# Node degrees of three chunks from the step tables instead of from products with a column of ones (graph network, one core)

## The reference

```
agg  = segment_sum(x[src], dst, num_segments=n)
deg  = segment_sum(ones_like(dst), dst, num_segments=n)
mean = agg / maximum(deg, 1)[:, None]
x    = mean @ Wl + x @ Wr + b
```

## Time and profile before

| what | us |
|---|---|
| median of 3 runs (lowest, highest) | 658.54 (657.63, 659.53) |
| the profiled execution's own time | 655.78 |
| its span in the profile | 653.9 |
| VectorE busy (share of the span) | 273.1 (42%) |
| ScalarE busy | 178.8 (27%) |
| layer 1: round 0 begins | 46.9 |
| round 1 begins | 102.8 |
| round 2 begins | 123.3 |

### The profile page before, as it was taken

How to read it: one execution, slowest core, us unless ns; L and a number is a source line. 1 busy time by engine, 2 the same in 40 slices (tenths; PEclk the granted TensorE clock), 3 DMA queues, 4 the chain that set the end, 5 groups by cost and what they waited for, 6 DMA issues and landing times.

```text
span 653.9 us, 10056 instructions
## 1 busy us (share of the span) xinstructions
PE 619.4 (95%) x4059; PEld 344.1 (53%) x4060; DVE 273.1 (42%) x514; ACT 178.8 (27%) x381; POOL 42.4 (6%) x93
## 2 busy tenths in 40 slices
PE   5769998899999899999999999899999999999998
PEld 4445555565555445554444444444446555646686
DVE  6978867589798779711121121121110110100011
ACT  3896853364644513210021011211110000000000
POOL 8003100000000000000000000000010011010110
PEclk9968999899999999999999999999999999999999
DMA  8401201510221112442435341355430213032030
GB/s 262 101 2 51 77 1 48 152 40 6 69 49 46 35 43 66 50 137 65 145 92 155 82 124 40 74 145 124 112 114 1 76 49 113 2 111 92 21 113 33
DMA packets 63526, 50.98 MB, mean 78 GB/s; under 512 B 35511, under 2 KB 48348, under 8 KB 63481
## 3 DMA queue, kind: packets, MB, share of 16 engines
q1 hardware_dynamic: 63124, 49.74, 27.0%
q0 software_dynamic: 240, 0.37, 0.2%
q10 hardware_dynamic: 116, 0.24, 0.1%
HBM read 28.15 MB, written 16.60 MB: 68 GB/s over the span
## 4 chain that ended last, share of the span: by engine, by line
PE 77%; DMA 8%; DVE 5%; ACT 5%; issue 2%; SPq 2%; POOL 1%; DVEq 0%; ACTq 0%; POOLq 0%
PE agg_ps L2254 27%; PE window_ps L2254 18%; PE lin_ps L2172 6%; PE lin_ps L2189 5%; PE window_ps L2085 4%; PE lin_ps L2148 3%; DMA rdeg_d<-newH 3%; PE lin_ps L2042 2%; DMA rdeg_d<-rdeg 2%; PE window_ps L2230 2%; PE agg_ps L2230 2%; ACT counts L1807 2%; DMA newH<-rdeg_d 1%; PE lin_ps L2276 1%; PE lin_ps L2197 1%
## 5 line engine op out<-in xcount | busy, mean ns | idle before, releaser
L2254 PE MATMUL agg_ps<-counts,H 128*128 128x512 f16 (+3 forms) x1026 | 234.9, 355 | 0.9 <-DVE aggT L1550 0.8
L2254 PEld LDWEIGHTS agg_ps<-counts,H 128*128 128x128 f16 (+1 forms) x1026 | 79.1, 98 | 55.9 <-issue 10.1
L1807 ACT ACTIVATE counts<-window_ps 128x400 f16<-128x400 f32 x150 | 73.6, 507 | 64.4 <-PE window_ps L2085 49.6
L1452 DVE TENSOR_TENSOR counts<-early 128x2048 f16<-128x2048 bf16 x66 | 78.0, 1215 | 6.6 <-PE window_ps L2085 5.1
L2254 PE MATMUL window_ps<-counts,early 128*128 128x512 f16 (+2 forms) x346 | 77.6, 379 | 0.0
L2254 PEld LDWEIGHTS window_ps<-counts,early 128*128 128x128 f16 (+1 forms) x346 | 33.7, 98 | 41.5 <-issue 3.4
L2254 PE MATMUL window_ps<-counts,H 128*128 128x512 f16 (+2 forms) x291 | 55.3, 346 | 0.0
L1550 DVE SCALAR_TENSOR_TENSOR aggT<-agg_ps,columns,rdeg 128x512 f32<-128x512 f32 (+1 forms) x27 | 17.0, 659 | 79.8 <-PE agg_ps L2254 63.1
L2085 PEld LDWEIGHTS window_ps<-counts 128*128 128x128 f16 x412 | 30.7, 99 | 34.6 <-issue 4.7
L1452 DVE TENSOR_TENSOR early<-early 128x1024 f16<-128x1024 bf16 (+1 forms) x69 | 43.9, 684 | 6.8 <-PE window_ps L2085 5.4
L2254 PE MATMUL agg_ps<-counts,early 128*128 (+4 forms) x297 | 46.5, 314 | 0.0
(11 more groups left out here) (251 smaller groups left out, 640.7 us busy)
## 6 DMA issues: line engine op xcount, KB each, us to landing
selfT<-hT_d SPq DMA_DIRECT2D x18, 512.0 KB, 4.3
hT_d<-newT SPq DMA_DIRECT2D x12, 512.0 KB, 4.5
rdeg<-rdeg_d SPq DMA_DIRECT2D x22, 256.0 KB, 4.2
counts<-in_x_dram SPq DMA_DIRECT2D x6, 512.0 KB, 7.9
hT_d<-counts SPq DMA_DIRECT2D x6, 512.0 KB, 3.3
newH<-in_x_dram SPq DMA_DIRECT2D x6, 512.0 KB
out_dram<-newT SPq DMA_DIRECT2D x5, 512.0 KB
hT_d<-newT SPq DMA_DIRECT2D x6, 256.0 KB, 4.0
```

Source lines behind the costliest of these rows:

```text
L1452: v.tensor_tensor(hots_of(group).rearrange("p r a (n d) -> p r a n d", d=2), pairs.unsqueeze(1).unsqueeze(1).broadcast_to([P, n, 2, P // 2 ...
L1807: a.activation(counts[:, :, 2 * w * WIN:2 * (w + 1) * WIN].rearrange("p t (a w) -> p a t w", a=2), window_bank(FILL_AT[w])[:, 0:2 * KEYS]. ...
L2254: last = m((agg_ps, window_ps)[bank][:, h, 0:n], tile[:, part, h * P:(h + 1) * P], counts[0:rows_, k, chunk_cols(c, n)], start=first and p ...
```

## The change

Places 0 to 2 take the way of the others: their degrees come from the step tables too. `add_degrees`, `degrees`, `turn_degrees` and `copy_degrees` are removed. The comparisons of place 0 are made at the start of round 0 and summed at its index 1, those of places 1 and 2 late in round 0, into rows of `counts` that are free then. The row now has one partition only (partition 32 of the `plan` tile), and all seven chunks are stored as a row and loaded as four neighbouring nodes on a partition, so that a piece has 16 bytes (4 bytes for the chunk of 53 nodes). `rdeg` is loaded only when the sums of the place before have been scaled. On SyncE the way of place 0 goes between the first h0 stores, that of place 1 to the head of `after(0)`, and that of place 2 into `after(1)`. GpSimd clears the row where it cleared `rdeg`.

```diff
-    BY_STEPS = 3
+    FROM_PARTS = 3
+        degree_row = plan_all[32:33, :].bitcast(f32)
...
+        early_cuts = [row(19, CH, CUT_SLOT), row(19, CH + CUT_SLOT, WTAIL * (WIN + 1)), row(20, CH, CUT_SLOT)]
...
-                def turn_degree_row(q):
...
+                def store_degree_row(q):
+                    c = ORDER[q]
+                    n, t = size_of(c)
+                    sp.wait_ge(degrees_taken, q + 1)
+                    sp.dma_start(rdeg_d[0:1, c * CH:c * CH + n], row_of(q)).then_inc(degree_row_stored, 16)
+                    sp.wait_ge(degree_row_stored, 16 * (q + 1))
+                    sp.dma_start(rdeg_columns[0:n // t, q, 0:t], degree_columns(q)).then_inc(degree_columns_loaded, 16)
+                def degree_columns(q):
+                    c = ORDER[q]
+                    n, t = size_of(c)
+                    return rdeg_d[0, c * CH:c * CH + n].rearrange("(p t) -> p t", t=t)
+                def store_rdeg(q):
+                    n, t = size_of(ORDER[q])
                     sp.wait_ge(degree_inverted, q + 1)
+                    sp.dma_start(degree_columns(q), rdeg_columns[0:n // t, q, 0:t]).then_inc(rdeg_columns_stored, 16)
+                    sp.wait_ge(rdeg_columns_stored, 16 * (q + 1))
+                    if q > 0:
+                        sp.wait_ge(agg_scaled[1], 2 * q)
+                    c = ORDER[q]
+                    sp.dma_start(rdeg[:, 0:n], rdeg_d[0:1, c * CH:c * CH + n].broadcast_to([P, n])).then_inc(rdeg_back, 16)
...
                     if l == 1 and not last:
                         double_tail(q + 1)
+                        if q == 0:
+                            store_degree_row(1)
+                            store_rdeg(1)
...
                         store_new(q)
-                        if l == 1 and BY_STEPS <= q + 1 < NCH:
-                            turn_degree_row(q + 1)
+                        if l == 1 and 2 <= q + 1 < NCH:
+                            store_degree_row(q + 1)
+                            store_rdeg(q + 1)
...
                     double_tail(0)
-                    for j in range(3):
+                    for j in range(2):
                         store_h0T(j)
+                    store_degree_row(0)
+                    store_h0T(2)
+                    store_rdeg(0)
                     load_self(0)
...
-                    sp.wait_ge(degree_inverted, BY_STEPS)
-                    for q in range(BY_STEPS):
-                        store_rdeg(q)
...
+            g.memset(degree_row, 0.0).then_inc(row_cleared, 1)
+            pool.wait_ge(row_cleared, 1)
...
-                    dve.wait_ge(rdeg_back, 16 * (q - BY_STEPS + 1)) if q >= BY_STEPS else dve.wait_ge(rdeg_made, q + 1)
+                    dve.wait_ge(rdeg_back, 16 * (q + 1))
...
-            first_round = {0: lambda: (h0_moments(3), bases_late(2)), 1: lambda: (degrees(0), h0_low_part(2)),
+            first_round = {0: lambda: (cut_steps(0), h0_moments(3), bases_late(2)), 1: lambda: h0_low_part(2),
+                           2: lambda: take_degrees(0),
...
+                           12: lambda: h0_low_part(4), 13: lambda: h0_shift(5), 14: lambda: invert_degrees(0),
+                           15: lambda: h0_low_part(5), 17: lambda: (cut_steps(1), cut_steps(2)),
...
-            second_round = {0: bound_h1, 2: bound_h2, 3: lambda: (add_own(0), plan_low()), 4: bound_h3, 15: lambda: low_part(1, 0, 0),
+            second_round = {0: lambda: (take_degrees(1), bound_h1()), 2: bound_h2, 3: lambda: (add_own(0), plan_low()),
+                            4: lambda: (bound_h3(), invert_degrees(1)), 15: lambda: low_part(1, 0, 0),
...
             def turn_bases():
                 pe.wait_ge(bases_made, 1)
+                pe.wait_ge(degrees_taken, 1)
...
-            def add_degrees(q):
...
-            def turn_degrees(q):
...
+            first_round = {1: lambda: sum_cuts(0), 3: lambda: turn_bases(), 4: lambda: h0_turn(2), 7: lambda: own_products(2),
...
-                if q < BY_STEPS:
-                    add_degrees(q)
-                else:
-                    if q < NCH - 1:
-                        sum_cuts(q)
+                if 0 < q < NCH - 1:
+                    sum_cuts(q)
+                if q > 1:
                     pe.wait_ge(low_done[1], q - 1)
...
                     if q == 1 and k == H0_LATE_K:
-                        pe.wait_ge(rdeg_made, 1)
+                        pe.wait_ge(degrees_taken, 2)
```

More of the change, by code:

```diff
@@ L985, in _ @@
                 after(1)
-                if l == 1:
-                    for q in range(2, NCH - 2):
-                        after(q)
-                    sp.wait_ge(degree_inverted, BY_STEPS)
-                    for q in range(BY_STEPS):
-                        store_rdeg(q)
-                elif l < 4:
+                if l < 4:
                     for q in range(2, NCH - 2):
@@ L1093, in _ @@
                                          ).then_inc(rows_gathered[i], 16)
-            for q in range(BY_STEPS, NCH):
-                pool.wait_ge(agg_scaled[1], 2 * q)
-                g.memset(rdeg[:, :], 0.0).then_inc(rdeg_cleared, 1)
+            for q in range(2, NCH):
+                pool.wait_ge(degree_row_stored, 16 * (q if q > 2 else 1))
+                g.memset(degree_row[:, 0:CH], 0.0).then_inc(row_cleared, 1)
             pool.wait_ge(late_loaded, LATE)
@@ L1504, in note @@
+                    v.tensor_reduce(out=degree_row[:, (CH if place == 1 else 0):][:, bass.ds(at, WIN)],
+                                    in_=degree_ps[32:33, 0:KEYS].rearrange("p (t w) -> p w t", w=WIN), axis=AX.X,
                                     op=ALU.add).then_inc(heavy_noted, 1)
                 for c in DUE[q]:
-                    if ORDER.index(c) < BY_STEPS:
-                        heavy_windows(dve, c, regs, rounds)
-                    else:
-                        heavy_windows(dve, c, regs, lambda w, first, n: (rounds(w, first, n), note(c, w)))
+                    heavy_windows(dve, c, regs, lambda w, first, n: (rounds(w, first, n), note(c, w)))
@@ L1636, in _ @@
                         first_round[k]()
-                    if 1 <= q < BY_STEPS and k == DEGREE_K:
-                        degrees(q)
-                    if BY_STEPS <= q + 1 < NCH - 1 and k == CUT_AHEAD_K:
+                    if FROM_PARTS <= q + 1 < NCH - 1 and k == CUT_AHEAD_K:
                         cut_steps(q + 1)
@@ L1861, in high_part @@
                     act.wait_ge(narrow_done, q + 1)
-                    if q + 1 >= BY_STEPS and q + 1 < NCH:
-                        act.wait_ge(cuts_summed, q + 2 - BY_STEPS)
+                    if FROM_PARTS <= q + 1 < NCH:
+                        act.wait_ge(cuts_summed, q + 2)
                 else:
@@ L1937, in _ @@
                         continue
-                    if k == DEGREE_COPY_K and q < BY_STEPS:
-                        copy_degrees(q)
                     if k == RELU_K:
@@ L2294, in sum_cuts @@
                 last.then_inc(cuts_summed, 1)
-            def turn_degrees(q):
-                n, t = size_of(chunk_at(q))
-                rows_ = P if n == CH else n
-                pe.wait_ge(degree_inverted, q + 1)
-                if q >= 1:
-                    pe.wait_ge(rdeg_made, q)
-                for i in range(t):
-                    last = m(degree_ps[:, i * P:i * P + rows_], rdeg_columns[0:rows_, q, i:i + 1].broadcast_to([rows_, P]),
-                             ident32[0:rows_, 0:rows_], start=True, stop=True)
-                last.then_inc(degree_turned, 1)
             def pick_rows():
@@ L2365, in _ @@
                     if kind == "lin":
+                        if q == 1 and k == 0:
+                            pe.wait_ge(own_copied, 2 * IN_LIN)
                         lin_part(q - 1, k)
```

161 lines of the change are left out of this document (56 added, 105 removed).

## The result

The changed kernel takes 666.88 us (median of 4 runs, 666.24 to 667.27), the kernel before 659.03 beside it (4 runs, 657.63 to 660.96): ratio 1.0118, interval 1.009 to 1.0146. It is slower, by 7.85 us, and the time lies above the range.

A forecast was written before the change was run, and what follows sets the result against it. TensorE was taken to set the pace, busy 619.4 of 653.9 us. Terms +2.6 + 0.5 - 0.9 - 1.3 + 0.8 = +1.7 us on the median 658.54 gave 660.2; range 654.5 to 665.

The forecast's parts named there:

- The price of the 53-piece store: SyncE, round 1: column store of 53 4-byte pieces takes 3.1 us at 13 ns a piece, bounds 2.45 and 10.45.
- second rival: SyncE's queue, round 1: small store costs by the transfer, 7.9 us, round 2 begins 4.8 later, 666.3 us; chance 0.18.
- Round 0: Products and turning go, VectorE's first one-hot pair sets the start: round 1 begins 1.6 us earlier, bounds 0.9 to 3.8.
- The fourth h0 store: SyncE ahead of round 2: first store lands in 3.0 us, three more add 3.8, fourth landed at 126.5.
- Round 1 up to the inversion: VectorE: bound operations run 13.6 us without a break from 101.75; inversion behind them done at 115.5.
- The clock after the stand: TensorE, start of round 2: half rate after standing some 8 us costs 0.5 us more, between 0 and 1.6.
- Rounds 2 to 6: Later rounds: turning goes -0.9, late-store waits go -1.3, round 2 waits for its columns +0.8 us.
- The turning: TensorE, round 2: turning a degree column into a row goes, -0.9 us.
- both go: -1.3: TensorE waits of 0.7 in round 4 and 0.6 at the last inversion vanish with shorter column stores; bounds 0 and -2.5.
- The 0.8 that round 2 was to get: Round 2: VectorE stands before the inversion until columns are back, costing TensorE +0.8 us, 0 to 1.5.
- first rival: Round 2 start: h0 stores in time, removed products' time comes out, sums begin 5.0 earlier, 652.1 us; chance 0.2.
- third rival: Rounds 0 to 2: windows with too many edges would run their own counts now; no change; chance 0.02.

The follow-up runs named there:

- row_before_h0: Changed kernel with only the degree row of place 0 stored ahead of the h0 of places 0 to 2: 663.88 us, ratio 1.0039.
- pieces_of_16: Changed kernel with place 1's degrees moved as 14 pieces of 16 bytes instead of 53 of 4 bytes: 661.39 us, ratio 0.9987.
- both edits: Changed kernel with place 1 as 14 pieces of 16 bytes and its inverted-degree store behind the four h0 stores: 654.11 us, ratio 0.9875.
- layout-alone kernel: Kernel before, with only the columns of places 3 to 6 as four neighbouring nodes a partition; products with ones stay: 656.78 us, ratio 0.9938.
- inverted_early_16: Changed kernel with 14 pieces of 16 bytes for place 1, its inversion before the first self addition, place 0's row before h0: 652.79 us, ratio 0.9809.

## Why the prediction was wrong, point by point

The path up to round 2's first sum and its order were right. That sum came 10.0 us later than forecast, through four terms that were sized too small (9.6 together; the rest is mostly the 2.9 from the landing to the sum, forecast 2.6). The length behind it, -1.1 us for a forecast of -0.9 (+0.5 - 0.9 - 1.3 + 0.8), agrees by luck.

**The price of the 53-piece store: 3.1 forecast, 6.4 measured (+3.3).** The step that failed is "by the piece, ... 13 ns". The price isn't linear in the pieces: 53 and 64 of 4 bytes cost 6.4 each, 512 cost 7.9 to 10.5, and 14 or 128 of 16 bytes 1.3 to 1.4. So "near the single piece, as 53 is nearer 1 than 512" interpolated between two points of which one, the single row of 2 KB, was of another kind. This is the second rival, with its place, its threshold (over 3.4 us) and its time, 666.3, close to 666.88. That closeness is luck: it held 4.8 for the store, which cost 3.3, and nothing for the three terms below. And its second half, that the new stores of 128 pieces stay slow too, was wrong. With that goes the rule that was weighed there (the Trainium skill, DMA: Bandwidth & Descriptors, "Specifications", a read-modify-write below 512 B): as the only rule it would make 4 and 16 bytes alike, and here they differ by a factor of 4 to 5. The other rounds' stores took 1.4 to 2.5 from issue to next issue in the changed kernel, instead of the forecast's 4.2.

**Round 0: 1.6 earlier forecast, 1.1 later measured (+2.7).** VectorE's first pair set the start, as forecast (50.15 for 49.6). The step that failed is the one from there to "round 1 begins 1.6 earlier": behind the first pair the next wait was ScalarE's, because its register load took 3.19 instead of at most 1.27 beside the h0 stores. The prediction had bounded this term by VectorE alone and had not asked what the earlier first sum releases on SyncE. With the stores moved (row_before_h0) round 1 begins at 101.79, 1.05 before the old 102.84: two thirds of the 1.6. The other third, with the degree products at half clock as forecast, was not split further.

**The fourth h0 store: 6.8 after the first issue forecast, 9.05 measured (+2.25).** The step that failed is "one such store lands in 3.0 at the least". That row was of stores issued far apart. Four in a row share the queue from the start; the first takes 5.2, which was the upper end of the earlier trace rows and the bound that the prediction named, and 5.2 + 3 x 1.28 is 9.04. With pieces_of_16 the first took 4.3, and the fourth landed at 8.2, again 3 x 1.28 more. The upper bound was the row of the same kind: it belongs to the pair issued 0.6 us apart at the start of round 0. That other stores behind them lengthen it was tried and is not so. The changed kernel's DMA issue of 127.10, last number from issue to landing, and its line 793 over all seven stores:

```profile
hT_d<-counts SPq DMA_DIRECT2D x1, 512.0 KB, 5.2
```

```profile
DMA to landing us min/median/max: 3.2/5.2/6.9
```

**Round 1 up to the inversion: 14.3 forecast, 15.6 measured (+1.3).** The step that failed is that the bounds run "without a break" for 13.6: TensorE ran at its lower level at the start of round 1, and VectorE waited for its products.

```profile
111.90 0.69 DVE L1584 TENSOR_TENSOR newT<-lin_ps,selfT 128x512 f32<-128x512 f32 x1 [0.85 <-PE lin_ps L2155]
```

Stretches as in the earlier trace rows; the third one is round 2's start:

```profile
105.00:108.00 3.00, 3.00 (x16) 2.94 (x16) 2.26 (x6) 1.17 (x3) 0.00 (x0) 0.50 0.05 7
...
130.00:136.00 6.00, 0.00 (x0) 0.00 (x0) 0.00 (x0) 0.00 (x0) 0.00 (x0) 0.50 1.03 394
...
139.00:142.00 3.00, 2.94 (x14) 1.56 (x15) 1.60 (x3) 0.87 (x2) 0.00 (x0) 0.50 0.27 98
```

At full clock the new round 1 takes what was forecast: with both edits (eight h0 transposes in 1.09 us) it is 14.3 from its begin to the inversion (105.05 to 119.39). The low clock isn't peculiar to the change. The layout-alone kernel, with the old round 1, shows it too (1.97), and two kernels with the new one don't (the one with both edits, and inverted_early_16). But nine of the eleven traces with the new round 1 have some of it between 100 and 110, and one of the two with the old; whether the change makes it more frequent was not tested. The execution profiled before had full clock there. The span grew by 11.5 and the median by 7.85 because that execution lay 3.25 below its median and the one profiled after 0.4 above; how much of the 3.25 is the clock isn't shown.

**The clock after the stand: +0.5 forecast, nothing to be seen.** TensorE stood for 13.7 us, the granted clock was 0.50 by 130, and it stayed at 0.50 for 3 us of work, until 142; before, it was some 3.4 us of 126 to 130. A longer stand did not make the start slower. The trace agrees with the Trainium skill (TensorE: Matmul & The Clock Gate, "What's actually happening"): "the default state is throttled, and activity releases the throttle".

**Rounds 2 to 6: -1.4 forecast (-0.9 - 1.3 + 0.8).** The turning came out as forecast: from round 2's first sum to the degree products of round 3 it is 33.7 us (139.06 to 172.8), before 34.7 (126.46 to 161.20). The step that failed is "both go: -1.3". Both waits stand in the changed kernel, as long as before:

```profile
PE turn_ps L2087 <- DVE early L1471: 0.7, 1, 0.7
PE lin_ps L2155 <- DVE aggT L1571: 0.6, 1, 0.6
```

The layout-alone kernel has them too, so the late stores weren't their cause; what is was not tried. The 0.8 that round 2 was to get has no wait in the trace, and round 3's 0.8 went. So up to the first sum of round 6 the changed kernel took 2.05 less (126.46 to 274.95 before, 139.06 to 285.50 now). Round 6 gave 1.7 of this back up to its wait of 0.6 (274.95 to 306.22, and 285.50 to 318.46), as TensorE fell to its lower level there (stretches as in the earlier trace rows, before and after, at the same place of the round):

```profile
285.50:289.50 4.00, 4.00 (x21) 1.78 (x19) 0.56 (x1) 0.00 (x0) 0.00 (x0) 1.00 0.96 345
...
296.00:300.00 4.00, 4.00 (x13) 1.50 (x12) 0.60 (x1) 0.00 (x0) 0.00 (x0) 0.60 1.01 313
```

The last 0.7 came behind that wait. Apart from the turning none of this is a term of the forecast, and only the sum agrees.

**The first rival (products' time comes out)** was wrong for this kernel, and its condition was the right one: "they would have to be issued by 112". Where the experiments meet it, with the store at 108 to 110 and the h0 stores from 110.63, the time goes to 0.981 and 0.976 of the kernel before, which is more than the rival's 0.990 (652.1 of 658.54); in the traces the spans are 4.5 and 3.3 below that of the kernel before (649.4 and 650.6 for 653.9). What the change removes was worth having; it was lost in the place of one 0.12 us operation on VectorE, in 4-byte pieces, and in a store that met a register load.

**The third rival** left no sign: the trace of the changed kernel has none of the products and sums of such counts. It was not tried by an experiment.

## What to carry to other kernels

When a change sends a small result through DRAM, put the operation that produces it at the point where its input lands, not where it is convenient in the engine's list: everything behind it in the DMA queue inherits its delay. Give such a store pieces of 16 bytes even if it must carry spare elements. And for each wait that goes, follow what it had been holding back on the queues; here an earlier sum started 1 MB of stores beside a register load and lost more than it had won.

## What the runs showed of the hardware that was not expected

- A store to DRAM of 4-byte pieces, one per partition, costs 6.4 to 6.9 us with 53 or 64 of them (7.84 right behind the h0 stores), and one of 16-byte pieces 1.27 (14 pieces; 2.9 right behind the h0 stores) to 1.44 (128; 3.03 once). The loads of the same layouts lie close together: 2.18 to 2.64 for 512 pieces of 4 bytes, 1.58 to 2.68 for 128 of 16.
- A register load on ScalarE took 3.14 to 3.19 us where stores of 512 KB ran beside it, and 1.53 to 1.56 where they didn't.
- Four stores of 512 KB issued in a row landed 8.2 to 9.4 us after the first issue in six traces, the first of them after 4.3 to 5.5; with nothing queued behind them it was 9.4.
- The same products at the start of round 1 ran at either level of the clock in different executions of the same code (1.09 or 1.97 us for eight transposes), worth about a microsecond.
